# A transformer block on one core: order of the first feed-forward pair, origin of the second pass's operands, place of the late transposes, and order of the last product

## The reference

```python
def _layernorm(x, axis=-1, eps=1e-05): return (x - mean) / sqrt(var + eps)
# attention: qkv = x @ Wqkv + bqkv; softmax(q @ k.T / sqrt(256)) @ v; @ Wo + bo
# feed-forward: y = silu(x @ W_gate.T) * (x @ W_up.T) @ W_down.T
x = x + _layernorm(attention(_layernorm(x)))
x = x + _layernorm(ffn(_layernorm(x)))
```

## Time and profile before

| what | value |
|---|---|
| runs | 1764.2 to 1769.44 us, median 1766.26 |
| the profiled execution | 1765.88 us, its span 1764.1 |
| PE busy | 1671.8 us, 95%, 7672 matmuls |
| weight loads of PE (beside its matmuls) | 1386.5 us, 79% |
| DVE busy | 1107.2 us, 63% |
| ACT busy | 628.6 us, 36% |
| POOL busy | 632.8 us, 36% |
| DMA | 268 MB, mean 152 GB/s |

### The profile page before, as it was taken

One profiled execution on the slowest core, in us unless ns is written; L12 is line 12 of the kernel. 1 busy time (PEld: TensorE's weight loads), 2 busy tenths in 40 slices (PEclk: granted clock), 3 DMA queues, 4 the chain that ended last, 5 costly groups with the idle time before them and its releaser, 6 DMA issues.

```text
span 1764.1 us, 20858 instructions
## 1 busy us (share of the span) xinstructions
PE 1671.8 (95%) x7672; PEld 1386.5 (79%) x7672; DVE 1107.2 (63%) x1613; ACT 628.6 (36%) x1135; POOL 632.8 (36%) x500
## 2 busy tenths in 40 slices
PE   7999999997699999999989999889999999999994
PEld 6788888876588888888868887668888888888883
DVE  7864777766966556555636766745555555644557
ACT  3223444444333233233336543323333233344441
POOL 4520455541654455444201102563455444200006
PEclk9999999998899999999989999989999999999997
DMA  7222466645223333332477665333223323487663
GB/s 277 108 83 72 144 208 210 218 147 214 79 102 105 123 114 114 126 131 94 135 258 255 208 202 191 131 125 114 90 90 110 129 96 111 137 284 237 193 195 126
DMA packets 117937, 268.32 MB, mean 152 GB/s; under 512 B 10320, under 2 KB 22736, under 8 KB 115280
## 3 DMA queue, kind: packets, MB, share of 16 engines
q1 hardware_dynamic: 117840, 267.05, 44.6%
HBM read 189.93 MB, written 77.08 MB: 151 GB/s over the span
## 4 chain that ended last, share of the span: by engine, by line
PE 84%; DVE 7%; DMA 3%; POOL 3%; issue 1%; ACT 1%; SPq 0%; POOLq 0%; DVEq 0%; ACTq 0%
PE ps L279 25%; PE ps L280 25%; PE ps L281 25%; PE ps L1719 3%; PE ps L1612 2%; DVE slots L1129 2%; PE ps L1720 2%; PE ps L1664 1%; POOL y_all L789 1%; DMA res<-x_dram 1%; DVE xc L1129 1%; DMA w_raw<-wffn 1%; PE ps L1665 1%; DMA x1n_tall<-x1n_dram 1%; DVE norm_y_stats L1545 1%
## 5 line engine op out<-in xcount | busy, mean ns | idle before, releaser
L1129 DVE TENSOR_TENSOR slots<-w_raw,slots 128x512 fp32r<-128x512 f32 x440 | 361.4, 849 | 314.2 <-ACT slots L951 313.9
L279 PE MATMUL ps<-xc,slots 128*128 128x512 f32 x1208 | 475.8, 394 | 31.4 <-DVE xc L1129 12.2
L280 PE MATMUL ps<-xc,slots 128*128 128x512 f32 x1208 | 474.2, 393 | 0.0
L281 PE MATMUL ps<-xc,slots 128*128 128x512 f32 x1208 | 473.8, 392 | 0.0
L951 ACT CAST slots<-w_raw 128x512 fp32r<-128x512 f32 x440 | 258.9, 619 | 379.6 <-PE ps L281 351.2
L279 PEld LDWEIGHTS ps<-xc,slots 128*128 128x128 f32 x1208 | 229.2, 190 | 82.7 <-issue 18.0
L281 PEld LDWEIGHTS ps<-xc,slots 128*128 128x128 f32 x1208 | 229.3, 190 | 48.0
L280 PEld LDWEIGHTS ps<-xc,slots 128*128 128x128 f32 x1208 | 229.4, 190 | 47.4
L279 PE MATMUL ps<-slots 128*128 128x512 f32 x616 | 240.5, 391 | 0.0
L280 PE MATMUL ps<-slots 128*128 128x512 f32 x616 | 240.1, 390 | 0.0
L281 PE MATMUL ps<-slots 128*128 128x512 f32 x616 | 240.1, 390 | 0.0
(11 more groups left out here) (153 smaller groups left out, 2316.1 us busy)
## 6 DMA issues: line engine op xcount, KB each, us to landing
w_raw<-wffn SPq DMA_DIRECT2D x106, 512.0 KB, 4.8
w_raw<-hsp_dram SPq DMA_DIRECT2D x154, 256.0 KB, 2.7
hsp_dram<-hs SPq DMA_DIRECT2D x20, 1792.0 KB, 6.2
w_raw<-wdt_dram SPq DMA_DIRECT2D x88, 256.0 KB, 3.3
w_raw<-wffn SPq DMA_DIRECT2D x70, 256.0 KB, 3.5
wdt_dram<-tt SPq DMA_DIRECT2D x11, 1024.0 KB, 5.3
xc_raw<-xq_dram SPq DMA_DIRECT2D x9, 1024.0 KB, 8.0
x_res<-x SPq DMA_DIRECT2D x16, 512.0 KB, 3.5
```

The source lines that it names most:

```text
L279: pe.matmul(dst, stat(HIGH), mov(HIGH), start=first, stop=False, skip_group_check=reread)
L280: pe.matmul(dst, stat(HIGH), mov(LOW), start=False, stop=False, skip_group_check=reread)
L281: return pe.matmul(dst, stat(LOW), mov(HIGH), start=False, stop=last, skip_group_check=reread)
L1129: return dve.tensor_tensor(dst, src, high.bitcast(F32), ALU.subtract)
```

## The change

There are four parts.

1. *First pair of pass 0 reordered.* The order of all operands is now a list, `ORDER`, and a number is looked up in it. In pass 0 the products of the leftover columns and of pair 0 are mixed. The first seven slots' low parts and that of A11 are made by POOL. Loading and summing pair 0's weights stands one attention tile earlier; the split of S2 on DVE now stands after the slot of (1, 1).

```diff
+def gate_order(P_):
+    pairs = [(p, j) for p in range(PAIRS) for j in range(PRODS)]
+    rests = [("r", r) for r in range(4)]
+    if P_ == 0:
+        head = [("r", 0), ("r", 1), (0, 0), (0, 4), ("r", 2), (0, 5), ("r", 3), (0, 1), (0, 2), (0, 3), (0, 6)]
+        return head + pairs[PRODS:]
+    return rests + pairs
...
+def down_order(P_):
+    order = []
+    extra = [("d", (PRODS - 1) * KP + k, x) for k in range(KP) for x in (0, 1)] if P_ == 1 else []
+    for s in range(STEPS - KP if P_ == 1 else STEPS):
+        order += [("d", s, 0), ("d", s, 1)]
+        if P_ == 1 and s >= 4 * KP:
+            order.append(extra.pop(0))
+    return order
...
+            def pool_low(n):
+                pool.wait_ge(w_high, n + 1)
+                pool.tensor_tensor(operand(n, LOW), source(n), operand(n, HIGH).bitcast(F32),
+                                   ALU.subtract).then_inc(w_low, 1)
...
                 for place, key in enumerate(gate_order(P_)):
...
+                    post(P_, p, j)
+                    next_low(n)
+                    if P_ == 0 and p == 0:
+                        if j == 0:
+                            split_low(0, S3)
+                        if j == 4:
+                            last_attention_tile()
+                        if j == 5:
+                            split_low(0, S2)
```

```diff
+            def store_sums(p):
+                sp.wait_ge(t_ready, 4 * p + 4)
+                sp.dma_start(wgt_dram[:, p, :, :].rearrange("q p n -> p q n"), tt[:]).then_inc(wgt_stored, 16)
...
+            def load_operand(n):
+                P_, key = ORDER[n]
+                if n >= FIRST_DOWN[0] + RING:
+                    sp.wait_ge(w_low, n - RING + 1)
...
+                sp.dma_start(w_raw[:, tile_of(n), :], part).then_inc(tile_loaded[tile_of(n)], 16)
...
-            rstd_y(0, 0, 3)
-            pair_sums(1, 0)
-            rest_sum(1)
-            sum_y(0, 0, 2)
-            sum_y(0, 0, 3)
+            out_block(0, 0)
...
+            def pair_sums(p):
+                raw = 4 * pair_buffer(p)
+                pool.wait_ge(w_loaded[pair_buffer(p)], pair_loads(p) - 32 * (p % 2))
+                if p > 0:
+                    pool.wait_ge(wgt_stored, 16 * p)
```

```diff
+            def transpose_late(i, g):
+                p = 4 * i + 3 + g
+                if g == 0:
+                    pe.wait_ge(late_normed, i + 1)
+                pe.wait_ge(u2_done, p + 1)
+                transposes(4 * (p % 2) + 1, KH * g, res[:, 1, :], KH).then_inc(xq_ready, 1)
```

```diff
+            for b in range(TPB):
+                bank_free(1, PRODS - 1, b)
+                for k in range(KP):
+                    if b == 0:
+                        pe.wait_ge(w_low, step_alloc(1, (PRODS - 1) * KP + k, 1) + 1)
+                    mm = step_tile(1, PRODS - 1, k, b)
+                mm.then_inc(tile_done, 1)
```

More of the change, by code:

```diff
@@ L603, in _ @@
-            gates(1)
-            downs(1)
-            for T in range(2):
-                for i in range(TPB):
-                    store_out(1, T, i)
-            sp.wait_ge(out_stored, 16 * TILES)
+                    if p % 4 == 1:
+                        for g in range(2):
+                            store_xq(LNT + i, g, res[:, 1, cols(g, BLOCK)].rearrange("p (k t) -> p k t", k=KH))
+                if p == PAIRS - 2:
+                    spilled(0, KP - 3)
+                    for n in range(4):
+                        load_operand(FIRST_DOWN[0] + n)
@@ L609, in _ @@
+            for i in range(TPB):
+                store_out(1, 0, i)
+            for i in range(TPB - 1):
+                store_out(1, 1, i)
+            for h in range(HALF):
+                sp.wait_ge(y_summed, 15 + h + 1)
+                sp.dma_start(out[S - P:S, cols(h, BANK)], y_all[:, YC21 + h, TPB - 1, :]).then_inc(out_stored, 16)
+            sp.wait_ge(out_stored, 16 * (TILES + 1))
         @block.gpsimd
@@ L792, in rstd_y, with out_block @@
                 rstd(norm_y, 8 * P_ + 4 * T + i, i)
-            clear_rest(0)
-            gates(0)
+            def out_block(P_, T):
+                rstd_y(P_, T, 0)
+                for i in range(1, TPB):
+                    rstd_y(P_, T, i)
+                    sum_y(P_, T, i - 1)
+                sum_y(P_, T, TPB - 1)
+            clear_rest(0)
+            for p in range(PAIRS):
+                if p + 1 < PAIRS:
+                    pair_sums(p + 1)
+                if p > 0 and is_up(p - 1):
+                    hidden_sums(0, pair_k(p - 1))
+                if late_tile(p) is not None and p % 4 == 2:
+                    rstd(norm_l, LNT + late_tile(p), 0)
+            hidden_sums(0, KP - 1)
             for h in range(2):
@@ L953, in split_high, with next_high @@
+                act.copy(operand(n, HIGH), source(n)).then_inc(w_high, 1)
+            def next_high(n):
+                high_from[0] = max(high_from[0], n)
+                while high_from[0] < ALLOCS and (resident(ORDER[high_from[0]]) or
+                                                 RING_OF[high_from[0]] <= RING_OF[n] + SLOTS):
+                    high(high_from[0])
+                    high_from[0] += 1
+            high_from = [0]
             def split_high(P_, slot):
@@ L959, in split_high_half @@
                     act.wait_ge((s1_done, s2_done, s3_done, s4_done)[(S1, S2, S3, S4).index(slot)], 2 * P_ + h + 1)
-                elif P_ == 1 and slot == A22:
-                    act.wait_ge(tall_evicted, 2 * TPB)
                 elif h == 0:
@@ L1312, in low_slot, with next_low @@
             def low_slot(n):
-                if n < PASSES * PER:
-                    dve.wait_ge(w_high, n + 1)
-                    low(slots[:, n % SLOTS, LOW, :], source(n), slots[:, n % SLOTS, HIGH, :]).then_inc(w_low, 1)
+                dve.wait_ge(w_high, n + 1)
+                if n == SLOTS:
+                    dve.wait_ge(w_low, SLOTS)
+                low(operand(n, LOW), source(n), operand(n, HIGH)).then_inc(w_low, 1)
+            low_from = [SLOTS]
+            def next_low(n):
+                while low_from[0] < ALLOCS and (resident(ORDER[low_from[0]]) or
+                                                RING_OF[low_from[0]] <= RING_OF[n] + SLOTS):
+                    low_slot(low_from[0])
+                    low_from[0] += 1
             def split_low(P_, slot):
@@ L1408, in _ @@
             pt_split(last, 0, 0)
+            a_norm(last - 2)
             pt_split(last, 1, 1)
```

1008 lines of the change are left out of this document (516 added, 492 removed).

## The result

The changed kernel takes 1747.7 us in the median (1745.61 to 1750.55) against 1766.3: ratio 0.9894, 95% interval 0.9874 to 0.9915. It is faster, by 18.6 us (about 1%; the interval leaves out 1) where 43 were forecast, and outside the stated range of 1704 to 1741. The profiled execution took 1747.18 us, its span is 1745.4. The time lies inside the 1735 to 1751 of rival 3, but not for its cause: PE's list of waits has none for the operands in `slots` or `last_w`, and its timeline names no wait at all between 777.82 and 1137.47, where x and the operands of the downs are loaded.

The account below looks back on a forecast made before the run. PE, with work for 95% of the span, was taken as the bound, so gains came only from its stalls, slow restarts and tail: 4.1 + 11.5 + 17.0 + 10.6 = 43.2 off 1765.88, plus 0.4 for the median: 1723 us, range 1704 to 1741.

Parts of the forecast that it names:

- rival 3: Operand loads bind mildly in steps 44 to 65 and the x stretch: 1735 to 1751 us; chance 0.14.
- B: Late tiles in pass 0: idle and slow-clock transposes go, as transposes move inside the gates; gain 11.5 us, bounds 7.5 to 11.5.
- A: Attention's end and first pair: earlier sums and new order gain 4.1 us, bounds -2 to +13.
- C: Pass boundary: operands come singly without POOL sums between; 6.7 of 23.7 us lost stay, gain 17.0, bounds 7 to 23.7.
- D: Tail after PE's last matmul: last product goes tile by tile, 12.5 us left; gain 10.6, bounds 8 to 14.
- 4 us of margin: Late tiles' stretch: the added 1 MB stores of sums end 4 us before the next pair's sums.
- rival 1: First pair and pass boundary: stalls go wholly, +10 and +6.7 us more gain, 1706 us; chance 0.20.
- Rival 2: Pass boundary: the gap stays because DVE's norms and POOL's sum_y hold the slots; 1740 us; chance 0.08.
- rival 4: 256 KB loads served at 190 GB/s bind PE, slower than before: 1778 us; chance 0.06.

Follow-up runs that it names:

- experiment 1: Changed kernel with each late tile's load issued one pair earlier (end of pairs 1, 5, 9, 13); 1723.63 us, ratio 0.9739 to the kernel before.
- experiment 2: Changed kernel with DVE's late-tile statistics moved later in the same pair, after (p,5) and (p,6); 1724.17 us, ratio 0.9752 to the kernel before.
- experiment 3: Changed kernel with the late load issued ahead of the 1 MB store of the weight sums, same pair; 1730.76 us, ratio 0.9782 to the kernel before.
- experiment 4: Changed kernel with DVE's split of S2 ahead of the low part of the slot for (1,1); 1746.05 us, ratio 0.9867 to the kernel before.
- experiment 5: Experiment 4 plus the store of x1's last tile ahead of the store of pair 1's weight sums; 1743.83 us, ratio 0.9862 to the kernel before.
- experiment 7: Changed kernel with the norm of the first pass's last row tile after u3 at the pass boundary; 1743.52 us, ratio 0.9864 to the kernel before.
- experiment 9: Changed kernel with POOL's two S4 sums held until DVE has split A22 and S3; 1744.48 us, ratio 0.9865 to the kernel before.

## Why the prediction was wrong

**The step that failed is in B:** "Their loads and norms are issued a pair before, and PE has seven slots (19 us) in hand." The first half holds only as seen from PE's transposes: load and statistics stand in pair 2, the transposes in the pairs 3 and 4. It leaves out the load's first reader, which is DVE. Before, SP issued the load in pair 2 and DVE asked for it in pair 3; now both stand in pair 2. In the kernel before, SP issued the first of these loads at 515.24, and DVE took it up at 535.23, 20 us later, without a wait:

```profile
515.24 0.38 SPq L505 DMA_DIRECT2D res<-x_dram  x1
```

It landed 7.7 us after its issue, the quickest of the four 3.2. So the trace of before could have told that the load needs a distance of some us; now DVE asks 0.3 after the issue. The second half is true of operands and of nothing else. The seven slots cover a late operand; PE doesn't wait for a slot in the four places, but for `u3`, which DVE makes in its order in the same pair, between two products. The cover in that path is some 4 us: `u3` is due at 521.35 (experiment 1), and PE comes to (2,5) at 524.9 (529.91 less 5.02). With the 1.4 or so that DVE itself makes up, these are the 5.4 found above. A wait of 10.43 on DVE outlasts it. Experiments 1 and 2 show it by taking away either end; with the step mended the result is 1723.63 and 1724.17, where the forecast had 1723. That near match is partly luck, as A was 2.6 too high and C and D 3.9 too low. In B itself the mended kernel takes 598.3 from (0,6) to the end of the downs (488.09 to 1086.4), a gain of 9.4 where 11.5 were forecast. 593.3 are 218 products and 2.8 the transposes; of the 2.2 that are left, (0,6)'s own slow matmuls after its wait make 1.6, and eight first matmuls behind transposes, which take 0.31 instead of 0.23, the rest.

I also priced the stores of the sums at nothing, with "4 us of margin" before the next sums. That margin was used up four times, while PE is in the pairs 4, 8, 12 and 16: there POOL waits 6.1 to 6.5 for the store, 25.4 in all; PE has no wait for a slot, so these are covered by the operands' lead, as forecast. The store's cost lay elsewhere: in the queue ahead of the late load, 16.9 us by experiment 3, and ahead of the store of x1 for which S4 waits (experiments 4 and 5). So this is the second term of B that failed, one that was put at nothing.

**A was mis-sized.** The mechanism came out as forecast, wait by wait: before (0,5) 10.01 (forecast 9.5), before (0,2) 8.83 (9.2). By the forecast's own times (0,6) starts at 483.1; it started at 487.63, 4.5 later, and 3.0 of these are there already at the attention's last weighing. It starts 8.07 earlier than before and not 11: the new wait on the query tile is 1.68 and not 0.6, and the idle times alone (2.77, 2.35 and 7.03 before, 1.68, 0.88 and 1.20 now) differ by 8.4, so up to there nothing was saved of the 1.6 that I had put to a slow restart. 0.8 more come by (0,5), and 0.7 from (0,2) to (0,6). The wait before (0,6) itself, 2.86 for S4's split, is as forecast (3.3, from 479.8 to 483.1). Experiment 4 shows that the slot of (1,1) ahead of S2's split does hold (0,2), and also why rival 1 was priced too high: with that hold gone PE stands elsewhere in the pair, and of the 10 us of rival 1 come 1.6, with the store moved 3.9.

**C was right.** Of 23.7 I let 6.7 stand; 4.8 stay. The wait for `u3` was 2.90 (forecast 3.9); the profile puts it down to issue, and experiment 7, in which it goes and 4.2 us with it, shows what it was. No wait of 0.9 before (0,3) is seen. Rival 2 is out.

**D was right in kind, 2 low.** After PE's last matmul come the norm of tile 2 and POOL's sum of it, then the norm of tile 3, its two adds of half a tile on DVE and two half stores:

```profile
1737.25 2.34 POOL L883 TENSOR_TENSOR y_all<-y_all,last_res 128x1024 f32<-128x1024 f32 x1 [1.38 <-DVE y_all L1725]
...
1740.40 0.81 DVE L1725 TENSOR_SCALAR y_all<-ps,norm_y_moments,norm_y_rstd 128x512 f32<-128x512 f32 x1 [2.37 <-POOL norm_y_rstd L714]
...
1741.58 1.28 DVE L1748 TENSOR_TENSOR y_all<-y_all,last_res 128x512 f32<-128x512 f32 x2
...
1742.29 0.95 SPq L696 DMA_DIRECT2D out<-y_all  x2
```

POOL's sum of tile 2 holds the root of tile 3 until 1739.6, 4.6 after PE's end (forecast 4.5). The last tile is what I over-priced: from there root, norm and both adds take 3.3, to 1742.86, and the landing 2.5, where I had up to 4.5 and 3.5.

**Rivals 3 and 4 are out.** The stretch with three operands a step, in the columns of the earlier trace rows:

```profile
1645.00:1700.00 55.00, 55.00 (x244) 45.57 (x244) 42.20 (x68) 32.80 (x59) 0.00 (x0) 1.00 0.80 259
```

PE is busy throughout at the full granted clock, with 259 GB/s at a share of 0.80, and no wait for `slots` or `last_w` is in PE's list. The Trainium skill's rule in "DMA: Bandwidth & Descriptors", section "Measured", to batch to 1 MiB, didn't bite on these loads of 256 KB (the page's table is for DMAs that GpSimd issues; these are SP's). Three are issued in each step of 2.72 us and land some 4 us after issue (3.8 to 4.3), so several are in flight at once.

## What to carry to other kernels

A lead belongs to a path, not to an engine: for each wait that an edit moves on an engine, list what stands behind it there and count the lead of each consumer by itself, down to the shortest. Where a load and its use are moved, compare the distance of issue and use before and after in the order of the engines, and what a new transfer puts ahead of the load in the queue; the sum of PE's work is the same, and these two made the 24 us here. And a stall that is mended inside a chain of several (experiments 4, 5, 9) is mostly handed to the next one, so count the chain's end and not the wait.
